# Layer 0 attention on one core: the products with the values one step later in a hand-placed schedule

## What is computed

```python
c_kv = x @ W_DKV
k = (c_kv @ W_UK).reshape(b, t, h, hd)
v = (c_kv @ W_UV).reshape(b, t, h, hd)
q = (x @ W_UQ).reshape(b, t, h, hd)
...
scores = jnp.where(causal, scores, jnp.asarray(-jnp.inf, scores.dtype))
probs = jax.nn.softmax(scores, axis=-1)
ctx = jnp.einsum('bhqk,bkhd->bqhd', probs, v).reshape(b, t, d)
return ctx @ W_O
```

## Time and profile before

| what | us |
|---|---|
| median of 3 runs | 1942.63 (1941.71 to 1945.28) |
| the profiled execution | 1945.23 |
| its span | 1943.6 |

### The profile page before, as it was taken

One profiled execution on the slowest core, in us unless ns is written; L12 is line 12 of the kernel. 1 busy time (PEld: TensorE's weight loads), 2 busy tenths in 40 slices (PEclk: granted clock), 3 DMA queues, 4 the chain that ended last, 5 costly groups with the idle time before them and its releaser, 6 DMA issues. The chain is left out here.

```text
span 1943.6 us, 32399 instructions
## 1 busy us (share of the span) xinstructions
PE 1729.3 (89%) x11015; PEld 1131.9 (58%) x11015; DVE 1139.9 (59%) x2512; ACT 1050.0 (54%) x1443; POOL 1007.3 (52%) x763
## 2 busy tenths in 40 slices
PE   4889888887899999999999976888888888878998
PEld 3455555554688888888888763343343334326556
DVE  5665666663233534335344537988888888846345
ACT  2555555555633323233232323998889889885543
POOL 2344443342334444344343444998889889874202
PEclk7999999998999999999999986999999999988999
DMA  4333333322621211012011263232322223117347
GB/s 128 89 110 92 87 92 92 108 77 75 198 88 60 72 35 60 26 58 82 26 59 36 61 209 130 72 93 66 88 88 86 85 71 109 34 58 265 111 153 232
DMA packets 119263, 182.86 MB, mean 94 GB/s; under 512 B 14198, under 2 KB 73078, under 8 KB 119163
## 3 DMA queue, kind: packets, MB, share of 16 engines
q1 hardware_dynamic: 112812, 173.21, 29.3%
q10 hardware_dynamic: 5712, 6.29, 1.0%
q0 software_dynamic: 640, 2.10, 0.3%
HBM read 90.72 MB, written 39.91 MB: 67 GB/s over the span
## 5 line engine op out<-in xcount | busy, mean ns | idle before, releaser
L878 POOL TENSOR_TENSOR l_prob<-l_prob,l_bias 128x1024 f32<-128x1024 f32 x192 | 452.3, 2381 | 57.1 <-ACT l_prob L1036 56.3
L1323 POOL TENSOR_TENSOR f_hl<-f_full,f_hh 128x512 fp32r<-128x512 f32 x192 | 247.9, 1291 | 401.3 <-DVE f_hh L1361 273.6
L1098 DVE CUSTOM_DVE_ANT_0 l_slot<-l_slot,l_bias 128x512 f32<-128x512 f32 x512 | 339.5, 714 | 26.5 <-PE l_slot L1183 26.4
L1039 ACT ACTIVATE l_prob<-l_prob 128x1024 f32<-128x1024 f32 x256 | 273.1, 1076 | 0.1
L523 DVE TENSOR_REDUCE l_peak<-l_slot 128x2 f32<-128x256 f32 (+3 forms) x256 | 206.1, 821 | 111.0 <-PE l_slot L615 108.6
L1411 PE MATMUL f_ps<-f_hh,f_hi_h 128*128 128x512 f32 x1024 | 260.6, 390 | 3.3 <-ACT f_hh L1335 2.6
L1411 PE MATMUL f_ps<-f_hl,f_hi_h 128*128 128x512 f32 x1024 | 258.3, 389 | 0.0
L411 ACT ACTIVATE l_prob<-l_slot 128x1024 f32<-128x1024 f32 (+3 forms) x256 | 175.1, 706 | 94.9 <-PE l_slot L634 91.9
L1411 PEld LDWEIGHTS f_ps<-f_hh,f_hi_h 128*128 128x128 f32 x1024 | 191.9, 188 | 47.4 <-issue 3.3
L350 POOL TENSOR_SCALAR_AFFINE_SELECT l_prob<-l_prob 128x256 f32<-128x256 f32 x256 | 105.2, 417 | 212.9 <-ACT l_prob L411 210.1
L1411 PEld LDWEIGHTS f_ps<-f_hl,f_hi_h 128*128 128x128 f32 x1024 | 192.2, 188 | 39.9
(11 more groups left out here) (229 smaller groups left out, 2774.9 us busy)
## 6 DMA issues: line engine op xcount, KB each, us to landing
l_stacks<-l_parts SPq DMA_DIRECT2D x372, 128.0 KB, 2.6
f_raw<-in_L_ffn_h_w SPq DMA_DIRECT2D x16, 512.0 KB, 4.2
f_raw<-in_L_ffn_h_w SPq DMA_DIRECT2D x32, 256.0 KB, 2.6
e_w<-in_L_ffn_f SPq DMA_DIRECT2D x32, 256.0 KB, 2.9
l_bias<-ext SPq DMA_DIRECT2D x16, 448.0 KB, 8.4
attn<-l_out_sb ACTq DMA_DIRECT2D x9, 512.0 KB, 2.9
l_x_in<-in_L_attn_x SPq DMA_DIRECT2D x8, 512.0 KB, 3.9
xh<-l_xh SPq DMA_DIRECT2D x8, 512.0 KB, 2.6
```

The source lines that it names most:

```text
L878: return eng.tensor_tensor(probs(n), src, bias[:, h:h + 2, j * P:j * P + T], ALU.add)
L1039: act.activation(probs(n), probs(n), ACT.Exp).then_inc(p_exp.sem, 1)
L1098: ins = dve.tensor_tensor_reduce(src, src, bias[:, 4 * g + 2 * pr + a, t * P:t * P + T], 1.0, 3 * NEG, ALU.add, ALU.max, peak[:, g, a, pr, ...
L1323: pool.tensor_tensor(t.hl[layer % 2][:, o], t.full[:, n % 2], t.hh[layer % 2][:, o].bitcast(F32), ALU.subtract).then_inc(self.h_lo.sem, 1)
```

## The change

The last constant of the place of each `value` goes from 4 to 5, so all sixteen, and `heads_copy` with them, stand one step later. `heads_turn` and `heads_norm` go from 11 to 12 in the same way. The four `mix` events go from step 17 to 18, where they stand ahead of `qk` 0; `out` goes from 24 to 25 and `store` from 25 to 26. Nothing is added or removed. `v` (15), `x_turn` (12), `latent` (16), `qk` (18 and 21), the maxima and all probs and scores keep their steps.

```diff
-                off, s = later(8 * g + 2 * j + 4 + LAG)
+                off, s = later(8 * g + 2 * j + 5 + LAG)
                 placed[s].append(("value", off, TT * g + j))
                 if j == TT - 1:
                     placed[s].append(("heads_copy", off, g))
                     if g % 2:
-                        off, s = later(8 * g + 11 + LAG)
+                        off, s = later(8 * g + 12 + LAG)
...
-                          17: [("mix_turn", -1, 0), ("mix_copy", -1, 0), ("mix_high", -1, 0), ("mix_low", -1, 0)],
-                          24: [("out", -1, 0)], 25: [("store", -1, 0)],
+                          25: [("out", -1, 0)], 26: [("store", -1, 0)],
```

More of the change, by code:

```diff
@@ L197, in latent_attention @@
                           16: [("latent", 1, 0), ("latent_top", 1, 0), ("latent_low", 1, 0)],
-                          18: [("qk", 1, 0), ("qk_copy", 1, 0)],
+                          18: [("mix_turn", -1, 0), ("mix_copy", -1, 0), ("mix_high", -1, 0), ("mix_low", -1, 0),
+                               ("qk", 1, 0), ("qk_copy", 1, 0)],
                           19: [("qk_high", 1, 0), ("qk_low", 1, 0)],
```

## The result

The changed kernel took 1926.85 us (median of 5 runs, 1925.71 to 1932.99) beside 1942.84 for the kernel before: a ratio of 0.9921, with a 95% interval of 0.9905 to 0.9938. The forecast was 1926.2. On a second chip session it was 0.9940 (0.9927 to 0.9953), so the gain is 11 to 16 us, and part of the forecast's closeness is luck. One execution of a later run (e1_again) took 4970.4 us at a granted clock of 1.0; it counts in that run's median of 1929.30, its ratio leaves it out, and nothing on record tells why.

The account below looks back on a forecast made before the run. TensorE, in flight for 89% of the span, was taken as the bound. Terms -8.4 - 8.5 + 7.1 - 2.4 - 1.9 - 2.8 + 0.5 = -16.4 us took 1942.63 to 1926.2 (1920 to 1931, chance 0.55; whole range 1916 to 1942).

Parts of the forecast that it names:

- Value 15 behind v: At the six joints between batches, value 15's stop for GpSimd's masking goes: -8.4 us.
- The clock: The half-clock stretch behind the stop goes in five of six joints, 1.7 us each: -8.5 us.
- ScalarE's new order: Behind value 15, the copy of v holds up ScalarE's queue, adding TensorE waits of 1.18 us in six turns: +7.1 us.
- Steps 21 to 25: Value 2 behind qk 1 hides its copy, saving 0.35 us in each of seven turns: -2.4 us.
- x_turn: Value 13 directly ahead of x_turn covers its wait of 0.26 to 0.53 us: -1.9 us for six.
- the other steps: In the groups of eight steps, value 6 fills score 30's wait, score 31 waits instead: 0.4 a turn, -2.8 us.
- a term that was put at nothing: On GpSimd's queue, mix_low passes to stand before qk_low; values depending on masks are four steps off: no cost.
- The last joint: No x_turn or latent behind value 15 hides the copy of v there: +0.5 us.
- the first two: Clock falls anyway: 1934.7 us, chance 0.20; the same with ScalarE's queue costing 14.2 instead of 7.1: 1941.8, chance 0.13.
- The third: Wide exponentials in the groups lose their cover, 0.5 us in about 25 groups, +12.5: slower, 1947.2 us, chance 0.12.

Follow-up runs that it names:

- e1_again: The kernel of e1 run once more, beside the kernel before at 1946.21: median 1929.30 us, ratio 0.9923.
- e1: The kernel before with x_low in step 13 instead of 12, so GpSimd masks prob 31 first: 1931.66 us, ratio 0.9936.
- e2: The kernel before with ten useless TensorE turns of the identity ahead of value 15, filling the stop: 1940.55 us, ratio 0.9978.
- e4: The kernel before with the other fifteen values, heads_turn 0, out and store one step later, value 15 kept: 1938.88 us, ratio 0.9965.
- e3: The kernel before with only value 15 and its heads_copy 3, heads_turn 1 and mix events one step later: 1936.47 us, ratio 0.9957.
- e0: The changed kernel itself, run again on a second chip session: 1929.42 us, ratio 0.9940 to the kernel before.
- e6: The changed kernel with x_low in step 13 instead of 12: 1928.66 us, ratio 0.9936 to the kernel before.
- e7: The kernel before with x_low in step 13, heads_turn 1 in 17, mix events in 19, qk 1 in 22: 1939.81 us, ratio 0.9995.

## Why the prediction held, point by point

- **Value 15 behind v.** Right, to the place: the forecast had value 15 at 6.3 us from `x_turn` and the copy of `v` at 6.8; they stand at 6.33 and 6.82. The stop is worth 1.41 us a turn (e1 against e2), the -8.4.
- **The clock, -8.5, and ScalarE's new order, +7.1.** Right as a pair for one joint, wrongly split. From `x_turn` to the end of score 20 the terms gave 18.7 us; it is 18.6 (256.89 to 275.49), and was 20.58 in this turn, 0.1 less in the others. Prob 6 waits 0.56, where 0.62 was said. But of these 1.98 us the stop is 1.41 (e1 against e2) and the clock alone only 0.95 (e2), since waits for ScalarE that half clock had covered come up at full clock. By the runs the two terms read -5.7 and about +2.3 (1.41 + 0.95 - 1.98 = 0.38, six times). Of the 1.74 us of waits that the forecast listed behind value 15, the rows show about 1.1: nothing ahead of score 16, 0.2 for `o_sb`, 0.23 ahead of the maxima, 0.56 at prob 6 and 0.12 for prob 5's exponentials. The forecast's 0.58 against 0.28 for prob 2 compares a duration with a distance between starts; by starts it is 0.38 (269.14 to 269.52) against 0.28. Away from a joint a stretch at half clock costs more: 1.35 to 1.54 us (55.41 against 54.06 for turns with and without one in e4, 54.24 against 52.7 in e1_again). I also counted five joints of six, and in the profile all six were cured. And I took the stop for a sufficient cause; e4 shows that it is not.
- **Steps 21 to 25, x_turn, the other steps: -7.1 together.** This is the step that failed. From score 20 to the next `x_turn` the turn had 34.75 us and has 34.38: 0.37, in place of 1.1. The wait of `x_turn` is gone as said, and prob 0 waits 0.71 for the copy of x (that one was said). But `qk` 1 waits 0.35 for VectorE's reduction of score 19, and this comes from a term that was put at nothing (under the last joint), `mix_low` in its new place. VectorE's rounding for `qk` 0 now falls into GpSimd's 2.35 us for `mix_low`, takes 1.70 us in place of 0.73, and holds up the reduction behind it; this is so in all six turns. The kernel before has the two apart, and e4, where value 2 has moved too but `mix_low` hasn't, has no such wait. For the groups, score 31 waits where score 30 did: 36 waits of 10.3 us in all instead of 33 of 12.2. e4, which has only these moves, gives about as little, 0.25 a turn. The two engines around `qk` 0, before, then after:

```profile
278.45 2.38 POOL L344 TENSOR_TENSOR l_mixt<-l_mix_full,l_mixt 128x1024 fp32r<-128x1024 f32 x1 [2.57 <-DVE l_mixt L519]
281.01 0.73 DVE L510 CAST l_parts<-l_qk_full 128x1024 fp32r<-128x1024 f32 x1
...
272.09 2.35 POOL L344 TENSOR_TENSOR l_mixt<-l_mix_full,l_mixt 128x1024 fp32r<-128x1024 f32 x1 [2.93 <-DVE l_mixt L519]
273.29 1.70 DVE L510 CAST l_parts<-l_qk_full 128x1024 fp32r<-128x1024 f32 x1
```

- **The last joint, +0.5.** Right in kind: TensorE waits 1.19 us for the copy of `v`, where it waited 0.45, which is 0.7 more.
- **The sum.** For the attention the forecast gain was 2.9 us too large: -16.4 against -13.5. The joints gave 6 x 1.98 = 11.9, in place of 9.8; the rest of the turns 2.2, in place of 7.1; two further stretches of half clock (at 255.5, and the second half of the one at 378.5), which I had left in, 2.8. Against that, the third `x_turn` is at 97.67 instead of 94.75, 2.9 later, with a later first score and the new stretch at 71 us. That the forecast of the whole still came out within a microsecond is the 3.0 us of the untouched rest, which is luck.
- **The rivals.** In the profile the clock fell nowhere in the joints, so the first two are out. The third needed score 30 to go on waiting for the wide exponentials; value 6 covers it.

## What to carry to other kernels

A wait at one instruction is often the end of another engine's queue: here moving GpSimd's one 2.4 us operation behind a 0.4 us mask did as much as moving sixteen products and four chains. In a schedule with few buffers, shifting work mostly renames the waits, so walk the queue from a fixed event through every engine before and after the move. The walk held to 0.1 us over the joint as a whole; it was off in its single waits, and in the steps behind. Look too for operations of two engines that will newly run side by side: here they lengthened one of them. Price half clock by what it adds to the turn, not by the lost cycles, and compare turns of the profile as well as times.

## What the runs showed of the hardware

- TensorE's clock fell to its lower level behind idle time that is short against the stretch at half clock: 1.34 us with small waits around it, or 0.56 and 0.46 near each other (e3). The Trainium skill, page "TensorE: Matmul & The Clock Gate", section "What's actually happening", names a stretch in which the engine was idle as what brings the lower level; the joints of the kernel before do not agree, since TensorE was busy for 2.22 of the 3.70 us ahead of 269.3, where the clock fell. Filling the idle time with useless turns kept the clock whole in the joints (e2).
- The same stop was followed by half clock in six joints of six in one kernel and in one of six in another (e4), and in e3 the stretch came at the same place turn after turn once it had come. What decides is open.
- VectorE's rounding of 1024 columns makes hardly any way while GpSimd subtracts 1024 columns. In the first 500 us of the 14 profiles it began beside a running subtraction 30 times (six each in after, e0, e3, e6 and e7); all 30 took 1.59 to 1.72 us and ended about 0.55 us behind the subtraction. The other 362 took 0.68 to 0.85. What the two share isn't shown.
